# Variance scalings on VectorE, split powers, and new piece orders for four engines in a fused four-layer kernel

## The chip, the cores and the metric

The kernel runs on one core of one Trainium2 chip. The metric is the device time of one execution in microseconds (us), lower is better. Engines are named as the profile names them: PE (TensorE matmuls), PEld (its weight loads), DVE (VectorE), ACT (ScalarE), POOL (GpSimd), SP (SyncE, which issues most of the DMAs).

## The reference

Sixteen sequences of 256 rows and 256 columns go through four layers, each followed by a layer norm of the sum of the layer's input and its output:

```
x = _layernorm(x + _L0_attn_ref(x, ...))   # state-space layer: projections, chunked decay scan, gate, W_out
x = _layernorm(x + _L0_ffn_ref(x, ...))    # int weights minus 128, times a scale; silu(gate) * up, down
x = _layernorm(x + _L1_attn_ref(x, ...))   # below
x = _layernorm(x + _L1_ffn_ref(x, ...))    # top 4 of 16 experts, softmax weights
...
qkv = _rms(x) @ w_qkv.T
q, k, v = jnp.split(qkv, 3, axis=-1)
q = _rms(q)
k = _rms(k)
w = jnp.exp(k)
kv_cum = jnp.cumsum(w * v, axis=1)
w_cum = jnp.cumsum(w, axis=1)
y = jax.nn.sigmoid(q) * (kv_cum / (w_cum + 1e-06))
uv = y @ w_swiglu.T
u, g = jnp.split(uv, 2, axis=-1)
return x + u * jax.nn.silu(g) @ w_out.T
```

## The kernel before

Three blocks run one after the other: the **layers** (three layers and the routing of the fourth, one sequence after another), the **experts** (144 tiles of 128 gathered rows through the 16 experts), and the **combination** (the last layer norm). The change touches the layers only.

In the layers each engine has its own instruction stream, cut into named pieces. `run_skewed` issues the pieces in the order that the table `ORDER` gives for the engine, once per round; round i works on sequence i in the pieces A and F, on i+1 in the pieces with a "+", on i-1 in the pieces B, on i-2 in C and on i-3 in D ("D8+" is i-2, "A6-" is i-1). Rounds 3 to 14 are a hardware loop, the others are written out. The engines meet only through semaphores, so a piece that waits holds up everything behind it in its own stream. What the pieces hold, as far as they are spoken of:

- **G1, G2, G3, G4** (sequence i+1): the first projections (PE), their copies and activations (ACT; G4 is the Silu into `xs`, G3 a logarithm), and the step sizes (DVE; G4.0, G4.1, G4.2 end in `d_a`, `ld`, `q`).
- **A2, A2R, A2L, A3, A3L, AV**: angles `ang`, the sum `g` (which POOL needs for `xg`), rotation, decay factors, masks. On POOL, A2 makes `xg` (128x1024), SP stores it, **AX.0** and **AX.1** gather four and three row selections back into `xgs`, and A2L starts `y`.
- **AU.n, A4.n, AY.n** (n = 0 to 7): one level of the scan each; DVE makes `u` (AU), PE multiplies by the mask (A4), DVE scales the product into `v` (A4) and adds it to `y` (AY, two instructions).
- **A5, A6, A6L**: squares of `y` (ACT), the power on POOL, gating on DVE, transposes and output projection on PE, statistics and normalised rows `x1` (A6L, line 1379).
- **F3, B1, B2**: gate projection `z`; the quantised layer: B1.j multiplies x1T by slices of `w_gate` and `w_up` into `pb`, ACT takes Silu into `sg`, DVE multiplies into `hT` (line 1385); B2 is the down projection. B1T, B3T and B5T are transposes of rows.
- **B2 and B2L** on DVE and POOL: sum `r2`, mean and variance `mv2`; POOL makes two scalings of the variance and one power over both (lines 1078 to 1081); DVE writes `x2n` and `x2` (line 1401). POOL's B3 makes the roots for q and k and negates the one for q (line 1088), which ACT uses as the scale of an exponential.
- **B3, B3V, B4, B5, B6, B6L**: the third layer; B5.j and B6 are its wide projections, B6L writes `x3`.
- **C7, C7L, C8**: `x3` split into two bf16 halves (POOL), logits, the best four experts (DVE, ending in `chosen`), counts (PE's C8), weights and slots (DVE's C8); D8 scatters them to memory (POOL, eight DMAs).
- **WH.k, WL.k**: pieces of the experts' weights, split into high and low halves (ACT, DVE) and stored by SP, one expert per round.

## Time and profile before

| | us |
|---|---|
| median of 3 runs | 2051.54 (2042.37 to 2051.62) |
| the profiled execution, its own time | 2046.18 |
| its span, first to last instruction | 2044.3 |

What the layers, experts and combination take of the span: to about 1427 us the layers, to about 1970 the experts, then the combination. The profile comes in several views: busy time of each engine in a stretch, with the granted TensorE clock (1.00 is 2.4 GHz, 0.50 is 1.2 GHz), and timelines, in which the number in square brackets is how long the engine stood idle before an instruction and who ended that. A timeline merges neighbouring instructions of a kind; "x2" is how many. A matmul in float32 shows as two records.

### The profile page before, as it was taken

What the parts mean: (1) busy time and instruction counts of PE and PEld (TensorE: products, weight loads), DVE (VectorE), ACT (ScalarE), POOL (GpSimd) and SP (SyncE); (2) the same over time, 40 slices, a digit from 0 to 9 for tenths busy, and PEclk for the clock granted to TensorE, in tenths of its full rate; (3) what the DMA queues carried; (4) which work ended last, traced back from release to release, by engine and by line L of the source; (5) the groups of instructions that cost most, each with busy time, mean ns of one, the idle gap of its engine ahead of it and who ended that gap; (6) DMA issues with size and microseconds to landing.
All of it is one profiled execution on the core that took longest, in us unless ns stands there. A gap on an engine that the chain in (4) does not pass through costs nothing. (4 is left out here: it accounts for less than half of the span.)

```text
span 2044.3 us, 34756 instructions
## 1 busy us (share of the span) xinstructions
PE 1763.1 (86%) x8580; PEld 1215.4 (59%) x8581; DVE 1328.9 (65%) x3020; ACT 730.0 (36%) x1384; POOL 854.8 (42%) x855
## 2 busy tenths in 40 slices
PE   3589999999999899998999998873889999999980
PEld 2257667666576676665766766653455566666650
DVE  4678878788788787787888887522344444444445
ACT  3234344344343443444434434221222233232323
POOL 2023243332432433334324333222466676776754
PEclk7799999999999999999999999977899999999995
DMA  5423132231331322313313223162999999999997
GB/s 201 148 94 106 35 110 72 77 109 39 99 109 29 109 70 78 109 39 99 108 30 114 72 71 105 31 273 96 230 158 153 168 172 168 168 171 167 172 142 249
DMA packets 369672, 242.79 MB, mean 119 GB/s; under 512 B 250640, under 2 KB 348240, under 8 KB 369232
## 3 DMA queue, kind: packets, MB, share of 16 engines
q1 hardware_dynamic: 303824, 170.22, 31.5%
q0 software_dynamic: 40704, 67.40, 17.2%
q10 hardware_dynamic: 25088, 4.50, 1.2%
q8 instruction: 26, 0.43, 0.1%
q14 instruction: 30, 0.25, 0.0%
HBM read 121.33 MB, written 68.78 MB: 93 GB/s over the span
## 5 line engine op out<-in xcount | busy, mean ns | idle before, releaser
L1675 PE MATMUL pu<-w_all,xh 128*128 x1728 | 364.3, 358 | 56.4 <-DMA xh<-xin 40.2
L1675 PEld LDWEIGHTS pu<-w_all,xh 128*128 128x128 bf16 x1728 | 169.2, 99 | 209.2 <-issue 92.2
L1806 POOL DMA_INDIRECT sums_dram<-yo,meta_in x144 | 227.8, 1582 | 140.2 <-issue 71.6
L1758 DVE TENSOR_TENSOR hid<-pu,gate 128x448 f32<-128x448 f32 x144 | 89.9, 625 | 255.8 <-PE pu L1675 133.9
L838 PE MATMUL pb<-x1T,w_sw 128*128 128x256 f32 x1024 | 231.2, 384 | 0.7 <-ACT x1T L956 0.7
L838 PEld LDWEIGHTS pb<-x1T,w_sw 128*128 128x128 f32 x1024 | 194.2, 192 | 46.2 <-issue 15.5
L1690 PE MATMUL py<-w_all,hh 128*128 x1584 | 198.4, 275 | 3.0 <-DMA hh<-hs 3.0
L1690 PEld LDWEIGHTS py<-w_all,hh 128*128 128x128 bf16 x1584 | 156.1, 99 | 45.3 <-issue 4.2
L1793 POOL DMA_INDIRECT xin<-x_dram,meta_in x144 | 142.2, 988 | 65.4 <-issue 47.0
L652 PE MATMUL pa<-w_in,xT 128*128 128x512 f32 (+1 forms) x384 | 154.5, 547 | 9.2 <-DMA bc_bias<-in_bc_bias 8.5
L1327 DVE SCALAR_TENSOR_TENSOR y<-v,small,y 128x512 f32<-128x512 f32 x224 | 157.7, 745 | 1.2
L1736 ACT ACTIVATE hs<-hid 128x448 bf16<-128x448 f32 x144 | 83.0, 576 | 197.2 <-DVE hid L1758 160.1
L1143 POOL DMA_INDIRECT meta_dram<-meta,slot x128 | 131.7, 1029 | 49.2 <-issue 43.1
L1727 ACT ACTIVATE gate<-pu 128x448 f32<-128x448 f32 x144 | 78.2, 543 | 194.2 <-PE pu L1675 143.6
L1108 POOL DMA_INDIRECT xgs<-xg_dram,chosen_rows x112 | 115.1, 1028 | 55.3 <-issue 34.4
L1044 POOL TENSOR_SCALAR yss<-yss 128x2 f32<-128x2 f32 x16 | 3.6, 225 | 310.2 <-ACT sq_a L943 310.2
L734 PE MATMUL pa<-u,masked 128*128 128x512 f32 x224 | 113.5, 613 | 19.6 <-DVE masked L1277 14.6
L996 ACT ACTIVATE sg<-pb 128x256 f32<-128x256 f32 x128 | 49.0, 383 | 203.7 <-PE pb L838 201.6
L1773 DVE TENSOR_SCALAR yo<-py,meta_in 128x256 f32<-128x256 f32 x144 | 69.6, 483 | 74.9 <-PE py L1690 44.7
L1314 DVE TENSOR_TENSOR v<-pa,decay 128x512 f32<-128x512 f32 x128 | 84.9, 684 | 51.1 <-PE pa L734 48.6
L652 PEld LDWEIGHTS pa<-w_in,xT 128*128 128x128 f32 x384 | 74.1, 197 | 71.2 <-issue 55.6
L847 PE MATMUL pb<-w_so,hT 128*128 128x256 f32 x512 | 113.1, 379 | 0.0
(244 smaller groups left out, 3196.3 us busy)
## 6 DMA issues: line engine op xcount, KB each, us to landing
w_stage<-in_w_ug SPq DMA_DIRECT2D x64, 224.0 KB
split_ug<-w_parts SPq DMA_DIRECT2D x64, 224.0 KB
w_all<-split_ug SPq DMA_DIRECT2D x16, 896.0 KB, 9.8
xg_dram<-xg SPq DMA_DIRECT2D x16, 512.0 KB, 3.5
w_stage<-in_w_dn SPq DMA_DIRECT2D x32, 256.0 KB
split_dn<-w_parts SPq DMA_DIRECT2D x32, 256.0 KB
w_all<-split_dn SPq DMA_DIRECT2D x16, 512.0 KB, 10.8
rows<-sums_dram SPq DMA_DIRECT2D x32, 256.0 KB, 5.4
```

Of the source, the lines that this page charges most:

```text
L652: last = mm(pa[:, bank + t, 0:width], xT[:, c, t * P:(t + 1) * P], w_in[:, c, first:first + width], start=c == 0, stop=c == DC - 1)
L734: mm(pa[:, n % 2, :], weights, u[:, n % US, :], start=True, stop=True).then_inc(level_done.sem, 1)
L838: last = mm(pb[:, 1 + j % 2, w * T:(w + 1) * T], w_sw[:, c, o:o + P], x1T[:, c, :], start=c == 0, stop=c == DC - 1)
L847: last = mm(pb[:, 3, t * D:(t + 1) * D], hT[:, j, t * P:(t + 1) * P], w_so[:, j, :], start=j == 0, stop=j == SJ - 1)
L1108: nc.gpsimd.indirect_dma_start(out=xgs[:, k, :], out_offset=None, in_=xg_dram, in_offset=bass.IndirectOffsetOnAxis(ap=chosen_rows[:, k:k + ...
L1143: nc.gpsimd.indirect_dma_start(out=meta_dram, out_offset=bass.IndirectOffsetOnAxis(ap=slot[:, t, j:j + 1], axis=0), in_=meta[:, t, j, :], ...
L1327: vec.scalar_tensor_tensor(y[:, t, :], v[:, n % 2, :], small[:, o:o + 1], y[:, t, :], ALU.mult, ALU.add).then_inc(y_added.sem, 1)
L1675: last = mm(pu[:, 2 * b + w, 0:EH], xh[:, m % XS, DC * xp + c, :], w_ug[:, bass.ds(e, 1), wp, c, w * EH:(w + 1) * EH], start=n == 0, stop= ...
L1690: last = mm(py[:, m % 2, 0:D], hh[:, m % XS, b, :], w_dn[:, bass.ds(e, 1), wp, b % EJ, :], start=n == 0, stop=n == EB + EJ - 1)
L1758: vec.tensor_tensor(hid[:, :], pu[:, 2 * (m % 2), 0:EH], gate[:, :], ALU.mult).then_inc(hid_ready.sem, 1)
L1793: nc.gpsimd.indirect_dma_start(out=xin[:, b, :], out_offset=None, in_=x3_dram, in_offset=bass.IndirectOffsetOnAxis(ap=meta[:, m, 1:2], axis=0)
L1806: nc.gpsimd.indirect_dma_start(out=sums_dram[m % 2], out_offset=bass.IndirectOffsetOnAxis(ap=meta[:, m, 0:1], axis=0), in_=yo[:, m % XS, : ...
```

## The change

- The scalings of the three variances leave POOL: DVE adds the small constant (`statistics`) or makes both scalings (DVE's B2) right behind its own statistics, and POOL only raises to the power. For x2n and x2 POOL does two powers of two elements each, x2n's first, and signals each.
- DVE's B2L writes x2n only; x2 is a piece of its own, B2M.
- The columns of `w_qkv` that make q are negated once at the start (DVE, behind sequence 0), and POOL's negation in B3 is gone.
- DVE's `g` is a piece of its own (A2G); routing's slots stay in C8, its weights become C9; POOL's D8 still waits for both.
- Semaphores are merged (`weights_made`, `padding_stored`), so that a chain of its own (`dve_c`) for routing has one.
- ORDER is new for PE, ACT, POOL and DVE; SP's is the same. On ACT, G4+ stands behind B5.1 instead of ahead of B5T, G3+ between B5.4 and B5.5 instead of behind B5.7, and C7L ahead of A2S. On POOL, C7 comes first, A2L's `y` stands between AX.0 and AX.1, and G1+ behind D8+.

```diff
-DVE_G, DVE_A, DVE_B = 10, 10, 16
+DVE_G, DVE_A, DVE_B, DVE_C = 10, 11, 9, 9
...
-    "POOL": ("A6- A2 A2L AX.0 AX.1 C7 B2 G1+ B3 D8+ A5 B6"),
+    "POOL": ("C7 A6- A2 AX.0 A2L AX.1 B2 B3 D8+ G1+ A5 B6"),
...
-            def deviation(chain, norm, mv, s):
+            def deviation(norm, mv, s):
                 pool.wait_ge(norm[0].sem, norm[0].at(s))
                 carrier.take()
-                chain.step(nc.gpsimd.tensor_scalar(mv[:, :, 1:2], mv[:, :, 1:2], 1e-5, None, ALU.add))
                 nc.gpsimd.tensor_tensor(mv[:, :, 1:2], mv[:, :, 1:2], power[:, 0:NT].unsqueeze(2), ALU.pow
...
-                nc.gpsimd.tensor_scalar(scales[:, 0:NT], mv2[:, :, 1], 1.0, LN_EPS, ALU.mult, ALU.add)
-                pb_.step(nc.gpsimd.tensor_scalar(scales[:, NT:2 * NT], mv2[:, :, 1], 1.0 + RMS_EPS, RMS_EPS * LN_EPS,
-                                                 ALU.mult, ALU.add))
-                nc.gpsimd.tensor_tensor(scales[:, :], scales[:, :], power[:, :], ALU.pow).then_inc(norm2[1].sem, 1)
+                for o in (NT, 0):
+                    nc.gpsimd.tensor_tensor(scales[:, o:o + NT], scales[:, o:o + NT], power[:, 0:NT], ALU.pow
+                                            ).then_inc(norm2[1].sem, 1)
...
-                pb_.step(root_mean(pb_, qk_ss[:, :, :].rearrange("p t m -> p (t m)"), D, RMS_EPS))
-                carrier.take()
-                nc.gpsimd.tensor_scalar(qk_ss[:, :, 0:1], qk_ss[:, :, 0:1], -1.0, None, ALU.mult
-                                        ).then_inc(qk_rms_ready.sem, 1)
+                root_mean(pb_, qk_ss[:, :, :].rearrange("p t m -> p (t m)"), D, RMS_EPS).then_inc(qk_rms_ready.sem, 1)
...
+            def a2_g(s):
                 vec.tensor_tensor(g[:, :, :], ld[:, :, :], pa[:, 2, 0:2 * H].rearrange("p (t h) -> p t h", t=NT),
                                   ALU.add).then_inc(g_ready.sem, 1)
...
+                    vec.tensor_scalar(w_qkv[:, :, 0:D], w_qkv[:, :, 0:D], -1.0, None, ALU.mult).then_inc(weights_made.sem, 1)
...
+            def statistics(chain, src, stats, mv, norm):
+                chain.step(moments(chain, src, stats, mv))
+                vec.tensor_scalar(mv[:, :, 1:2], mv[:, :, 1:2], LN_EPS, None, ALU.add).then_inc(norm[0].sem, 1)
...
-                statistics(cb_, r2, st2, mv2, norm2)
+                cb_.step(moments(cb_, r2, st2, mv2))
+                vec.tensor_scalar(scales[:, 0:NT], mv2[:, :, 1], 1.0, LN_EPS, ALU.mult, ALU.add)
+                vec.tensor_scalar(scales[:, NT:2 * NT], mv2[:, :, 1], 1.0 + RMS_EPS, RMS_EPS * LN_EPS,
+                                  ALU.mult, ALU.add).then_inc(norm2[0].sem, 1)
+
+            def normalised_twice(s, o, to, done):
+                dve.wait_ge(norm2[1].sem, norm2[1].at(s, 2 if o == 0 else 1))
+                for t in range(NT):
+                    vec.tensor_scalar(to[:, t, :], r2[:, t, :], mv2[:, t, 0:1], scales[:, o + t:o + t + 1],
+                                      ALU.subtract, ALU.mult).then_inc(done.sem, 1)
```

What the new orders move is shown at three places of the loop's body. The first is DVE's stream at the start of a round: the angles, `g`, the rows x1 of sequence i-1 (`x<-r,mv`), and the search for the best experts from `top` to `chosen`. Before:

```order
L1238 TENSOR_SCALAR ang<-ang 128x128
L1239 TENSOR_TENSOR g<-ld,pa 128x128
...
L1379 TENSOR_SCALAR x<-r,mv 128x256 x2
L1250 TENSOR_TENSOR bct<-bcn,cs 128x256
...
L1260 TENSOR_TENSOR coef<-ld,cb 128x128
L1451 MAX top<-logits 128x8 x2
...
L1466 TENSOR_REDUCE chosen<-hot 128x32
```

The same stretch of the changed kernel:

```order
L1231 TENSOR_SCALAR ang<-ang 128x128
...
L1379 TENSOR_SCALAR x<-r,mv 128x256 x2
L1460 MAX top<-logits 128x8 x2
...
L1475 TENSOR_REDUCE chosen<-hot 128x32
L1234 TENSOR_TENSOR g<-ld,pa 128x128
L1245 TENSOR_TENSOR bct<-bcn,cs 128x256
...
L1255 TENSOR_TENSOR coef<-ld,cb 128x128
```

`g` and the whole rotation moved behind x1 and the search. On PE the counts that need `chosen` moved with it, from behind B1.0 to directly behind B1T.

The second place is PE around the transposes of x2n, B3T (line 757): line 790 is B2, line 734 the scan levels A4, line 652 G1+, line 803 the q and k projection. Before:

```order
L790 MATMUL pb<-w_down,hT 128x256 x7
L734 MATMUL pa<-u,masked 128x512
L734 MATMUL pa<-u,masked 128x512
L652 MATMUL pa<-w_in,xT 128x288 x4
L757 MATMUL pb<-ident,x2n 128x128 x4
L803 MATMUL pb<-w_qkv,x1T 128x512 x4
```

The same stretch of the changed kernel:

```order
L790 MATMUL pb<-w_down,hT 128x256 x7
L652 MATMUL pa<-w_in,xT 128x288 x4
L734 MATMUL pa<-u,masked 128x512
L757 MATMUL pb<-ident,x2n 128x128 x4
L734 MATMUL pa<-u,masked 128x512
L803 MATMUL pb<-w_qkv,x1T 128x512 x4
```

One of the two scan levels moved between the transposes and the projection that needs their copy.

The third place is PE at the end of a round: B5's last slices (line 838), B6 (line 847), the transposes of y, A5 (line 740), and the output projection A6 (line 746). Before:

```order
L838 MATMUL pb<-x1T,w_sw 128x256 x4
L847 MATMUL pb<-w_so,hT 128x256 x7
L847 MATMUL pb<-w_so,hT 128x256 x9
L740 MATMUL pa<-ident,y 128x128 x8
L746 MATMUL pa<-w_out,ynT 128x256 x8
```

The same stretch of the changed kernel:

```order
L838 MATMUL pb<-x1T,w_sw 128x256 x4
L847 MATMUL pb<-w_so,hT 128x256 x7
L847 MATMUL pb<-w_so,hT 128x256
L740 MATMUL pa<-ident,y 128x128 x4
L847 MATMUL pb<-w_so,hT 128x256 x8
L740 MATMUL pa<-ident,y 128x128 x4
L746 MATMUL pa<-w_out,ynT 128x256 x8
```

The first half of A5 moved between the halves of B6.

## Rows read from the trace of the kernel before

**Rows 1.** Windows: us, busy PE PEld DVE ACT POOL, then clock, DMA share, GB/s.
```profile
662.95:745.05 82.10, 76.33 (x331) 54.88 (x330) 65.21 (x146) 33.84 (x66) 29.05 (x33) 0.98 0.26 80
```
**Rows 2.** Timeline of DVE: the sum r1, once per round (start us, us, ...).
```profile
258.68 0.69 DVE L1341 TENSOR_TENSOR r<-x_row,pa 128x512 f32<-128x512 f32 x1 [0.74 <-PE pa L746]
...
1321.83 0.69 DVE L1341 TENSOR_TENSOR r<-x_row,pa 128x512 f32<-128x512 f32 x1 [0.74 <-PE pa L746]
```
**Rows 3.** Timeline of PE, one round: the places where it stood idle.
```profile
664.09 3.72 PE L746 MATMUL pa<-w_out,ynT 128*128 128x256 f32 x16 [0.31 <-ACT ynT L949]
...
674.41 0.66 PE L757 MATMUL pb<-ident,x 128*128 128x128 f32 x4 [0.49 <-DVE x L1379]
...
679.64 0.18 PE L867 MATMUL pb<-chosen,count_mats 128*128 128x16 bf16 x1 [0.84 <-DVE chosen L1466]
...
682.53 1.13 PE L776 MATMUL pb<-x1T,w_gate 128*128 128x256 f32 x4 [0.41 <-DVE hT L1385]
...
691.74 6.03 PE L790 MATMUL pb<-w_down,hT 128*128 128x256 f32 x24 [1.03 <-DVE hT L1385]
...
703.06 0.66 PE L757 MATMUL pb<-ident,x2n 128*128 128x128 f32 x4 [1.43 <-DVE x2n L1401]
704.40 5.40 PE L803 MATMUL pb<-w_qkv,x1T 128*128 128x512 f32 x8 [0.69 <-ACT x1T L956]
...
714.43 0.70 PE L820 MATMUL pb<-wv,const 128*128 128x256 f32 x2 [0.34 <-ACT eq L987]
```
**Rows 4.** Windows within that round, and timeline of PE in a later round.
```profile
705.02:706.04 1.02, 1.02 (x2) 0.34 (x1) 1.02 (x3) 1.01 (x3) 0.73 (x2) 0.50 0.00 0
...
1032.64 3.70 PE L803 MATMUL pb<-w_qkv,x1T 128*128 128x512 f32 x8 [0.69 <-ACT x1T L956]
```
**Rows 5.** Timelines of DVE and of POOL, the same round's start.
```profile
671.97 2.38 DVE L1379 TENSOR_SCALAR x<-r,mv 128x256 f32<-128x256 f32 x2
...
676.44 0.25 DVE L1451 MAX8 top<-logits 128x8 f32<-128x16 f32 x2
...
677.14 1.44 DVE L1457 TENSOR_TENSOR ez<-top 128x8 f32<-128x8 f32 x1
...
672.22 1.98 POOL L1095 TENSOR_TENSOR xg<-xs,g 128x1024 f32<-128x1024 f32 x1 [1.20 <-DVE g L1239]
676.60 1.96 POOL L1115 TENSOR_TENSOR y<-xs,coef 128x1024 f32<-128x1024 f32 x1 [2.40 <-DVE coef L1260]
```
**Rows 6.** Timelines of POOL and of DVE between the variance and x2n.
```profile
665.57 0.71 POOL L1051 TENSOR_TENSOR mv<-mv,power 128x2 f32<-128x2 f32 x1
...
699.52 0.25 DVE L1373 BATCH_NORM_AGGREGATE mv<-st 128x2 f32<-128x6 f32 x2
...
702.26 0.73 DVE L1401 TENSOR_SCALAR x2n<-r,mv,scales 128x256 f32<-128x256 f32 x2 [1.21 <-POOL scales L1081]
...
680.38 0.17 DVE L1479 TENSOR_SCALAR tok<-tok 128x2 f32<-128x2 f32 x1
```
**Rows 7.** Timeline of ACT in B1: the late sg.
```profile
690.69 0.83 ACT L966 ACTIVATE sg<-pb,s_gu 128x256 f32<-128x256 f32 x2 [3.93 <-PE pb L776]
```
**Rows 8.** Gathers: timelines of SP, of POOL, and of both POOL and DVE in round 0.
```profile
676.01 0.37 SPq L615 DMA_DIRECT2D xg_dram<-xg  x1
...
680.14 1.09 POOL L1108 DMA_INDIRECT xgs<-xg_dram,chosen_rows  x1 [1.58 <-DMA xg_dram<-xg]
...
39.74 0.95 POOL L1108 DMA_INDIRECT xgs<-xg_dram,chosen_rows  x1 [0.30 <-issue]
...
47.09 1.90 DVE L1305 TENSOR_TENSOR u<-xgs,from_first 128x512 f32<-128x512 f32 x3 [8.96 <-DMA xgs<-xg_dram,chosen_rows]
```
**Rows 9.** Timelines of ACT, DVE and PE at the round's end.
```profile
738.54 1.28 ACT L902 ACT_TABLE_LOAD   x1
...
742.83 1.41 DVE L1334 SCALAR_TENSOR_TENSOR y<-y,yss,zs 128x512 f32<-128x512 f32 x2
...
737.94 7.07 PE L847 MATMUL pb<-w_so,hT 128*128 128x256 f32 x32
```

More of the change, by code:

```diff
@@ L1394, in b2, with b2_second @@
                                            ALU.add))
[L1395 to L1402 removed]
+                cb_.step(moments(cb_, r2, st2, mv2))
[7 more added lines that the diff above has]
+                                      ALU.subtract, ALU.mult).then_inc(done.sem, 1)
+            def b2_late(s):
+                normalised_twice(s, NT, x2n, x2n_ready)
+            def b2_second(s):
+                normalised_twice(s, 0, x2, x2_ready)
             def b3(s):
@@ L1439, in b6 @@
                 statistics(cb_, r2, st2, mv2, norm3)
+                cb_.end()
             def b6_late(s):
@@ L1446, in c7_late @@
             def c7_late(s):
-                cb_.go_on(s)
+                cc_.start(s)
                 dve.wait_ge(logits_copied.sem, logits_copied.at(s))
@@ L1451, in c7_late @@
                     last = vec.max(top[:, t, :], logits[:, t, :])
-                cb_.step(last)
+                cc_.step(last)
                 carrier.take()
@@ L1463, in c7_late @@
                                              spread(topf[:, t, :], 2, NE), ALU.is_equal)
-                cb_.step(last)
+                cc_.step(last)
                 with nc.allow_low_precision(reason="sums of at most one one are exact"):
@@ L1469, in c8, with c9 @@
             def c8(s):
-                cb_.go_on(s)
+                cc_.go_on(s)
+                dve.wait_ge(counted.sem, counted.at(s))
+                cc_.step(vec.tensor_tensor(pos[:, :, :], pb[:, 3, 0:NT * NE].rearrange("p (t e) -> p t e", t=NT),
+                                           spread(base[:, :], 1, NT), ALU.add))
+                vec.tensor_tensor(base[:, :], base[:, :], pb[:, 3, NT * NE:(NT + 1) * NE], ALU.add)
+                for t in range(NT):
+                    last = vec.tensor_tensor(hot_pos[:, t, :, :], hot[:, t, :, :], spread(pos[:, t, :], 1, TOPK), ALU.mult)
+                cc_.step(last)
+                cc_.step(vec.tensor_reduce(slot_f[:, :, :], hot_pos[:, :, :, :], AX_X, ALU.add))
+                if later(s):
+                    dve.wait_ge(meta_stored.sem, meta_stored.before(s))
+                flat = "p t j -> p (t j)"
+                vec.scalar_tensor_tensor(slot[:, :, :].rearrange(flat), topf[:, :, :].rearrange(flat), float(cap),
+                                         slot_f[:, :, :].rearrange(flat), ALU.mult, ALU.add
+                                         ).then_inc(meta_ready.sem, 1)
+            def c9(s):
+                cc_.go_on(s)
                 dve.wait_ge(top_exp.sem, top_exp.at(s))
-                cb_.step(vec.tensor_reduce(esum[:, :], ez[:, :, :], AX_X, ALU.add))
-                cb_.step(vec.reciprocal(esum[:, :], esum[:, :]))
+                cc_.step(vec.tensor_reduce(esum[:, :], ez[:, :, :], AX_X, ALU.add))
+                cc_.step(vec.reciprocal(esum[:, :], esum[:, :]))
                 if later(s):
```

84 lines of the change are left out of this document (32 added, 52 removed), and 17 rows, old and new, of the table ORDER.

## The prediction

> **What bounds the kernel now.** I read first the windows. In one round of the layers, 82.10 us long, PE is busy 76.33 us and DVE 65.21, at a granted clock of 0.98 [rows 1]. So PE sets the round, and what can be won is what PE waits and what it loses at the lower clock. The sum r1 marks the rounds: from 258.68 to 1321.83 us there are 13, 81.8 us each [rows 2], and two more lie before them. The experts and the combination are not touched and have no piece of the layers beside them, so they move as a whole.
>
> Next the timeline of PE through one round, where the reader is to see every idle time and its releaser [rows 3]: 0.31 (ACT's copy of y's transposes), 0.49 (x1), 0.84 (`chosen`), 0.41 (the first `hT`), 1.03 (a late `hT`), 1.43 (x2n), 0.69 (the copy of x2n's transposes), 0.34 (the exponential of q): 5.5 us. Then the clock: right behind the 2.1 us of idleness around x2n the q and k projection takes 5.40 us, and the window inside it shows 0.50, that is 1.2 GHz; in a later round the same eight records take 3.70 at full clock [rows 3, 4]. That is 1.7 us more. It happens in 10 of the 13 rounds.
>
> **The change, part by part**, as us per round.
>
> *x1 and g.* Today `g` comes first, POOL's xg starts at 672.22 and lasts 1.98, and DVE's two x1 instructions take 2.38 instead of the 0.73 of the equal x2n pair [rows 5, 6]. With `g` behind the search, xg can't start there: x1 is ready 1.65 us earlier, PE's 0.49 goes. What is late next is PE's own gate projection. The price moves to the rotation, which then stands beside xg for up to 1.98 us. PE needs the rotated B and C only behind B1.1, two slices of eight 256-column records later; 0.43 us is a 512-column record at full clock (3.70/8 less its tail), so a slice is 1.73. That covers it: nothing.
> The row shows that a tensor_scalar of DVE stood still while POOL read SBUF. The Trainium skill (SBUF — State Buffer, Who interferes with whom) says the same of instructions of DVE with two SBUF inputs, and that who starts first keeps the port for the whole instruction; by it xg's and y's 2 us fall upon the rotation and on `u`, never away, and the gain would be nil if PE waited for those. The rows of this kernel say that it doesn't for the rotation; for `u` it is part of the second and third rivals.
>
> *`chosen`.* The search starts at 676.44, its `ez` takes 1.44 beside POOL's y, and PE waits until 679.64 [rows 3, 5]. Without that blocking (at least 1.2 us) it takes 3.2 - 1.2 = 2.0. Behind x1, from about 672.6, it ends near 674.6, when PE has done B1T (674.41 less 0.49 and 0.5 of work, 674.4). The 0.84 shrinks to 0.2 at most; ACT gets to the first `sg` earlier too (its table loads follow one another without the wait for `ez`), which takes the 0.41. Gain 0.84 + 0.41 - 0.2 = 1.05.
>
> *The late hT.* PE's 1.03 comes from an `sg` that ACT starts only at 690.69, 3.93 us after its last work, though its matmuls ended near 687.9 [rows 3, 7]. No piece ahead of it explains that; it coincides with the gathers. I keep the 1.03: bounds 0 (stays) and 1.03 (goes).
>
> *x2n.* From the variance (699.52 + 0.25) to x2n (702.26) it is 2.49 us: two scalings and one power over four elements [rows 6]. Now DVE adds two tensor_scalars on tiny operands, 0.17 each of which about 0.1 counts, with one step wait: 0.3. POOL wakes 0.2 later and needs 0.71 for a power over two elements [rows 6]: 1.25 in all. Gain 1.2 on the path to B3T. One scan level (0.86) leaves the cover ahead of B3T, so the 1.43 stays at about 1.1, but it comes to stand in the 0.69: from B3T to the projection the copy takes 704.40 - 703.06 = 1.34, of which 0.5 is transposes and 0.86 the level. So the projection starts 1.2 us earlier. x2 in its own piece costs nothing: only the next round's x1 and B6 read it.
>
> *The clock.* Idleness there falls from 2.1 to 1.1 us in one piece, with dense records on both sides. All other waits of the round, up to 1.03 us, left the clock at 1.00. I take the full 1.7 in the 10 rounds that have it; bounds 0 and 1.7.
> The Trainium skill (TensorE: Matmul & The Clock Gate, Part 1) describes a gate that rests at half rate and is released by activity. The trace agrees with two levels; by the rule alone a remaining 1.1 us wait may keep the fall; the sum would then be 3.4 a round, which is the first rival.
>
> *q's sign.* One POOL instruction and its step wait go from a chain that PE waits 0.34 for; two scan levels and B3V still cover it. Gain 0.34 [rows 3]. The negation at the start costs DVE about 0.4 us once.
>
> *The end of the round.* B6.0, A5.0, B6.1, A5.1, A6: ACT's copy of the first half now lies beside B6.1 (3.5 us), so the 0.31 goes. But the first half of y must be normalised by the end of B6.0. Today B6 starts at 737.94, half of its 7.07 ends at 741.5, and the gating starts at 742.83, done 0.7 later [rows 9]: 2 us too late. The new orders pull A4.7 and AY.7 ahead of B5.6 and of G4.1's reciprocal, put ACT's squares ahead of B5.7, and move G4.2 behind the gating. On DVE AU.7, AY.2 and AY.3 stand ahead of B5.0 and WL.4 behind A5, so that it has room. Counting DVE's and ACT's pieces from the exponential on, I get the gating about 0.5 us ahead of need. G3's logarithm now sits between two Silus, and costs ACT two table loads of 1.28 [rows 9] where one was; ACT is idle half of the time there.
>
> *The rest.* POOL's C7 first costs the x1 power nothing, since x3 is ready before x1's variance. POOL's eight scatters ahead of G1+ end some 2 us before DVE's G4.0 wants the root. SP's order is the same.
>
> Sum per round: 0.49 + 1.05 + 1.2 + 0.34 + 0.31 = 3.4, and 1.7 where the clock falls: 5.1. Over 15 rounds: 15 x 3.4 + 10 x 1.7 = 68. In the drain after 1321.83, where nothing covers the chains, x2n (1.2), the negation (0.3) and x3's scaling (0.3) give 2 us more. Each wait that goes takes the pipeline's tail with it (about 0.1, three us in all). From 2046.2 of the profiled execution (span 2044.3 and 1.9 around it): **1973 us**. The runs' median, 2051.5, is 5 above that execution; three rounds that kept the full clock in the one and lost it in the others are 3 x 1.7 = 5, and with the fall gone both start from the same place.
>
> **The rivals.**
> 1. *The clock still falls.* For: a wait of 1.1 remains at the same place. Against: it is half as long. 12 to 15 rounds x 1.7: 1973 + 20 to 25 = 1995.
> 2. *The end of the round becomes the bound:* y isn't gated by B6.0's end, or DVE, busy 65 of what would be 77 us, is late with `hT`. For: the margin of 0.5. Each us is 15: with 1.5, 1995; with the first rival, 2016.
> 3. *The gathers, slower than before.* xg ends 2.5 us later (near 676.8); from SP's issue to the first gather it was 4.1 us [rows 8], so AX.0 starts near 681.1 and its fourth issue (0.95 + 0.30 each) ends near 686. DVE's AU.0 comes at 687.5, ahead of B1.5, and PE's B2 wants that hT at 690.7, two `u` later. So data may land 3 us behind the last issue; with the port taken by y (1.96) that is about what is there. In round 0, beside the weights' loads, it was 47.09 - 40.69 = 6.4 [rows 8]: then PE waits 3.4 us per round, 51 us in all, 2024. It turns slower than before beyond 3 + 5 = 8 us; at 9 it gives some 2062. Against: in the loop the DMAs are at a quarter load.
> 4. *More is won:* the late `sg` goes as well, 15 x 1.03, and the tails count double: 1973 - 15 - 3 = 1955. That the change doesn't do what it says is excluded for the scalings (POOL's instructions are gone) and small for the rest.
>
> **How the numbers follow.** Forecast (1960 to 1988) 0.50; clock 0.18; end of round, alone or with the clock, 0.16; gathers late but still faster 0.04, slower 0.03; more won 0.09. The range goes from below the fourth rival to the second with the first, 1946 to 2016, and leaves out the late gathers and what no row told me of. A measurement here tells 0.5%, about 10 us, from no change. Faster by more: all but the gathers' slow part and a little unforeseen: 0.93; same 0.03, slower 0.04.
>
> **What would show it.** Right: r1's distance near 76.7 us; no 0.50 in the window of the q and k projection; x1 in 0.73 us; PE waits for `chosen` and ynT gone; x2n's wait near 1.1; B6's halves without a wait between. Wrong: DVE waiting for `xgs` ahead of B1.5, PE waiting for y at A5.0, or a new idle time of PE behind ACT's Silu at B5.5. A round of 79 or more would say that DVE or ACT took over.

## The result and the profile after

The changed kernel takes **1956.6 us** (median of 4, 1956.2 to 1958.5), the kernel before 2047.2 beside it (median of 4, 2042.4 to 2051.6): ratio 0.956, 95% interval 0.953 to 0.959. Forecast were 1973.0, with a range of 1946 to 2016.

The views of the changed kernel answer to the rows of before as follows. First its windows over one round (columns as in [rows 1]):

```profile
625.87:701.97 76.10, 74.48 (x330) 54.20 (x331) 64.51 (x150) 35.38 (x67) 28.59 (x29) 1.00 0.28 86
```

The round went from 82.1 to 76.1 us and PE's busy time from 76.33 to 74.48 at an unbroken clock. So of the 6.0 about 1.9 is busy time, 1.7 of it the clock's, and 4.1 is idle time. Next, PE's timeline from the end of B2 to the first scans, against the 1.43, 0.69 and 5.40 of [rows 3]:

```profile
653.36 2.21 PE L652 MATMUL pa<-w_in,xT 128*128 128x288 f32 x8
655.40 1.02 PE L734 MATMUL pa<-u,masked 128*128 128x512 f32 x2
657.45 0.66 PE L757 MATMUL pb<-ident,x2n 128*128 128x128 f32 x4 [1.02 <-DVE x2n L1403]
657.94 1.02 PE L734 MATMUL pa<-u,masked 128*128 128x512 f32 x2
658.80 3.69 PE L803 MATMUL pb<-w_qkv,x1T 128*128 128x512 f32 x8
```

The one wait that is left here is 1.02; the projection runs at full clock. The chain that ends it, on DVE and POOL, against [rows 6]:

```profile
655.18 0.25 DVE L1369 BATCH_NORM_AGGREGATE mv<-st 128x2 f32<-128x6 f32 x2
655.46 0.17 DVE L1396 TENSOR_SCALAR scales<-mv 128x2 f32<-128x2 f32 x1
655.54 0.16 DVE L1397 TENSOR_SCALAR scales<-mv 128x2 f32<-128x2 f32 x1
656.65 0.73 DVE L1403 TENSOR_SCALAR x2n<-r,mv,scales 128x256 f32<-128x256 f32 x2 [0.95 <-POOL scales L1076]
...
655.88 1.54 POOL L1076 TENSOR_TENSOR scales<-scales,power 128x2 f32<-128x2 f32 x2 [5.75 <-DVE scales L1397]
```

From the variance's end (655.43) to x2n it is 1.22 us; it was 2.49. The start of the round on DVE and PE, against [rows 3, 5]:

```profile
629.98 0.73 DVE L1379 TENSOR_SCALAR x<-r,mv 128x256 f32<-128x256 f32 x2
...
632.11 0.37 DVE L1475 TENSOR_REDUCE chosen<-hot 128x32 bf16<-128x128 f32 x1
...
632.92 2.20 DVE L1246 TENSOR_TENSOR bcu<-bcn,cs 128x256 f32<-128x256 f32 x1
...
632.54 0.18 PE L867 MATMUL pb<-chosen,count_mats 128*128 128x16 bf16 x1
```

x1 takes 0.73, `chosen` is there when PE gets to it, and the slow instruction beside xg is now one of the rotation, `bcu`, which nobody waits for.

To compare whole executions I cut them into rounds at the end of PE's last up projection of B1, and summed within each round the pauses between PE's records above 0.1 us (**waits**). What remains (**rest**) is work, at the clock it had. The first of these cuts is the **first mark**, the sixteenth is the last; 15 rounds lie between them, the first and the last of which are the outer ones. A **fall** is a stretch in which the granted clock is 0.50. The means of the 13 inner rounds, in us:

| kernel | round | waits | rest | first mark |
|---|---|---|---|---|
| before, first traces | 81.35 | 5.43 | 75.92 | 120.9 |
| after, first traces | 75.93 | 1.49 | 74.44 | 113.1 |
| before, with the experiments | 80.29 | 4.79 | 75.50 | 121.3 |
| after, with the experiments | 75.75 | 1.33 | 74.42 | 109.5 |

The rest is two-valued: in the trace of before with the experiments 76.3 in seven inner rounds and 74.6 in six, the 1.7 of [rows 3, 4]; after has 74.4 in all. In the first pair the 87.6 us of the spans are 13 x 3.94 = 51 of waits, 13 x 1.48 = 19 of rest, 7.8 up to the first mark, 7.7 in the two outer rounds, and 1.6 behind the last mark. Of these 1.6, 1.3 lie in the experts (559.0 to 557.7 us), whose code is the same; the layers' own part behind the last mark is as long as before (70.4 and 70.6).

### The profile page after: what moved, and what is told of

Read it like the earlier page. It is cut to its first block and busy times, and to the rows that moved or that the text cites. A ratio compares the mean times of both kernels' runs of the same rounds, so it can differ in the third digit from the quotient of the medians.

```text
span 1956.7 us, 34760 instructions
## 1 busy us (share of the span) xinstructions
PE 1740.7 (89%) x8580; PEld 1208.8 (62%) x8581; DVE 1320.4 (67%) x3085; ACT 751.6 (38%) x1398; POOL 844.3 (43%) x791
## 5 line engine op out<-in xcount | busy, mean ns | idle before, releaser
L652 PE MATMUL pa<-w_in,xT 128*128 128x512 f32 (+1 forms) x384 | 159.8, 562 | 23.5 <-DVE masked L1272 14.2
L1102 POOL DMA_INDIRECT xgs<-xg_dram,chosen_rows x112 | 122.1, 1091 | 93.0 <-DMA xg_dram<-xg 47.7
L652 PEld LDWEIGHTS pa<-w_in,xT 128*128 128x128 f32 x384 | 74.6, 201 | 84.7 <-issue 68.4
L776 PE MATMUL pb<-x1T,w_gate 128*128 128x256 f32 (+1 forms) x384 | 103.5, 392 | 0.8 <-DVE w_down L1360 0.4
L847 PEld LDWEIGHTS pb<-w_so,hT 128*128 128x128 f32 x512 | 95.0, 190 | 13.6
```

Source lines behind the costliest of these rows:

```text
L652: last = mm(pa[:, bank + t, 0:width], xT[:, c, t * P:(t + 1) * P], w_in[:, c, first:first + width], start=c == 0, stop=c == DC - 1)
L776: last = mm(pb[0:rows, 1 + j % 2, w * T:(w + 1) * T], weight[:, c, j * P:j * P + rows], x1T[:, c, :], start=c == 0, stop=c == DC - 1)
L847: last = mm(pb[:, 3, t * D:(t + 1) * D], hT[:, j, t * P:(t + 1) * P], w_so[:, j, :], start=j == 0, stop=j == SJ - 1)
L1102: nc.gpsimd.indirect_dma_start(out=xgs[:, k, :], out_offset=None, in_=xg_dram, in_offset=bass.IndirectOffsetOnAxis(ap=chosen_rows[:, k:k + ...
```

## The experiments

All runs beside the kernel before, which takes 2031 us there (2047 in the first comparison). "Control" is the changed kernel. e5, e6, e8 and e10 ran on another chip than the control and the other experiments; the kernel before takes 2032 there, 1.3 more, and the control was not run on it.

The experts' part, from its first matmul to its last, has the same code in all kernels and takes 548.9 to 559.3 us in the 14 traces. That puts a scatter of 10 us into the totals; its cause is open. So each total is read beside the time of the last mark, which only the layers set (one trace each, difference to the control in brackets): control 1251.3; e1 1269.8 (+18.5); e2 1299.6 (+48.3); e3 1291.4 (+40.1); e4 1264.3 (+13.0); e5 1254.1 (+2.8); e6 1301.0 (+49.7); e8 1254.7 (+3.4); e9 1261.7 (+10.4); e10 1341.4 (+90.1); before 1325.8; e7 1318.2.

### Controls

No edit.

> The changed kernel, unedited, beside the experiments on their chip, so that they are compared with it there. The kernel before takes 2031 us on the chip of the first four experiments against 2047 in the first comparison. Theory A (the difference between chips lies in how often the clock falls and how often the fifth sg comes late before): the changed kernel has neither and takes its 1957 us here too, within 4. Theory B (everything scales): 1957 x 2031 / 2047 = 1942 us.

> The kernel before, unedited, for a trace of it from the chip of the experiments. In the first trace the ten rounds with the clock's fall took 76.4 us without TensorE's waits and the others 74.8, and the fifth sg was over 2 us late in nine rounds. If this chip's 2031 us are the same rounds with fewer falls, about (2047 - 2031) / 1.6 = 10 rounds fewer fall, that is nearly none; if the late sg is what differs, TensorE's waits in the down product (0.9 us in those nine rounds) are gone and the falls stay.

Measured: after **1952.9** (ratio 0.963, 0.959 to 0.967), before 2029.5. The control's theory A holds: after moved by 4 us only, while before moved by 16. The trace of before shows both causes that its expectation names. It has the fall in 7 inner rounds where it had 9 of 13 in the first trace, and the late `sg` in none:

```profile
677.59 0.47 ACT L966 ACTIVATE sg<-pb,s_gu 128x256 f32<-128x256 f32 x1 [1.25 <-PE pb L776]
679.32 0.47 ACT L966 ACTIVATE sg<-pb,s_gu 128x256 f32<-128x256 f32 x1 [1.25 <-PE pb L776]
682.05 0.47 ACT L966 ACTIVATE sg<-pb,s_gu 64x256 f32<-64x256 f32 x1 [2.26 <-PE pb L776]
```

These are three Silus of ACT in one round, each right behind its matmuls; in [rows 7] the fifth one had waited 3.93. PE's wait for `hT` at B2, 0.73 in the mean of the inner rounds then, stands in two of them here (0.48 and 0.60). So with the same code the late `sg` comes in the first comparison and not here, and the same holds of after: 0.5 us late in eleven rounds of the first trace, never here. The record does not name the chip of the first comparison, so that a difference between chips is likely but not shown. Of the 16 us by which the two `before` differ, 13 x 0.64 = 8 are waits and 13 x 0.42 = 5 rest.

### e1: the arithmetic back on POOL

```
-                vec.tensor_scalar(scales[:, 0:NT], mv2[:, :, 1], 1.0, LN_EPS, ALU.mult, ALU.add)
-                vec.tensor_scalar(scales[:, NT:2 * NT], mv2[:, :, 1], 1.0 + RMS_EPS, RMS_EPS * LN_EPS,
...
+                nc.gpsimd.tensor_scalar(scales[:, 0:NT], mv2[:, :, 1], 1.0, LN_EPS, ALU.mult, ALU.add)
+                pb_.step(nc.gpsimd.tensor_scalar(scales[:, NT:2 * NT], mv2[:, :, 1], 1.0 + RMS_EPS, RMS_EPS * LN_EPS,
...
+                nc.gpsimd.tensor_scalar(qk_ss[:, :, 0:1], qk_ss[:, :, 0:1], -1.0, None, ALU.mult)
```

The other two variances' additions go back to POOL as well. What stays from the change is the split power, x2n's first, and x2 as a piece of its own.

> The changed kernel with its new orders, but the variance scalings, the additions of epsilon and the negation of q's factors done on GpSimd again, as before. Theory A (the arithmetic carries a part of the gain, the orders the rest): TensorE's wait for x2n is 1.02 us with the change; two or three GpSimd operations of 0.54 to 0.60 us and a power of 1.04 in place of 0.71 stand in the chain again, so it grows to about 2.2, that is 1.2 x 15 rounds = 18 us; q's sign gives back 0.34 x 15 = 5 us at the wait for eq; and if the longer wait takes TensorE's clock down again (query and key products 5.4 in place of 3.69 us) another 1.7 x up to 14 = 24. Sum +23 to +47 us over the changed kernel's 1956.6, that is 1980 to 2004. Theory B (the orders do it all, the chain of x2n has slack now): under +5 us, at most 1962, the wait for x2n as before this edit, and the products at 3.69 us throughout.

Measured: **1965.1**, 12.2 above the control; rounds of 76.68, waits 2.38, rest 74.31, no fall. Up to the last mark it is 18.5 more, and the experts take 6.2 less. So theory A without its clock part (23) is near in the sum. It is not in the terms: x2n's wait grew by 0.27 a round, not 1.2; two short waits at the start of the round (0.14, and 0.23 for ACT's `zs`) and 4.0 us ahead of the first mark were not in it. POOL and PE in one round:

```profile
661.24 0.19 POOL L1078 TENSOR_SCALAR scales<-mv 128x2 f32<-128x2 f32 x1 [5.66 <-DVE mv L1378]
661.49 0.19 POOL L1079 TENSOR_SCALAR scales<-mv 128x2 f32<-128x2 f32 x1
...
663.33 0.66 PE L757 MATMUL pb<-ident,x2n 128*128 128x128 f32 x4 [1.30 <-DVE x2n L1408]
...
673.11 0.70 PE L820 MATMUL pb<-wv,const 128*128 128x256 f32 x2 [0.44 <-ACT eq L987]
```

POOL's scalings take 0.19 each here, not 0.53 and 0.54. What stands beside them in the kernel before (its trace with the experiments, POOL and DVE):

```profile
690.17 0.53 POOL L1078 TENSOR_SCALAR scales<-mv 128x2 f32<-128x2 f32 x1 [7.80 <-DVE mv L1373]
690.77 0.54 POOL L1079 TENSOR_SCALAR scales<-mv 128x2 f32<-128x2 f32 x1
...
689.97 1.29 DVE L1305 TENSOR_TENSOR u<-xgs,from_first 128x512 f32<-128x512 f32 x2
```

Two wide `u` of DVE lay over POOL's small instructions. The new order took AU.4 and AU.5 out from between B2 and B2L. So the path to x2n was shortened three times: by the order, by the split power and by moving the scalings. The waits go from 1.43 + 0.69 = 2.12 to 1.29 in e1 (order and split power), to 0.49 + 0.69 = 1.18 in e2 below (split power and moved scalings), to 1.02 with all three. POOL's part up to x2n's power falls from 2.26 us to 1.26 in e1; 0.69 of that is the two scalings without `u` over them, 0.31 the power (1.04 over four elements, 0.73 over two). The order was not run alone against this wait: e1 still has the split power. The Trainium skill (SBUF — State Buffer, Who interferes with whom) has the shared port of DVE and POOL; these rows agree for a two-input instruction of DVE, 0.54 against 0.19. In these rows `u` had started 0.2 us ahead of POOL's instruction; where POOL's root starts 0.1 ahead of a `u`, in the control, it keeps its 1.01.
q's sign costs 0.44 at `eq` where I had 0.34.

### e2: the arithmetic alone, in the old order

The table `ORDER` of before, with DVE's `A2 A2G`, `C8 C9` and `B2L B2M` next to each other, so that each pair does what one piece did.

> The changed kernel's arithmetic (scalings on VectorE, x2n's power apart, queries negated once) in the order of pieces of the kernel before. Theory A (orders and arithmetic each carry their own part and add): the start of the state space part (x1 and the chosen rows, 1.3 us a round) and the late sg (about 0.9 us in 10 rounds) come back, 15 x 1.3 + 10 x 0.9 = 29, the first round's wait for the weight pieces 5.5, sum +34 us, 1991; where the clock falls again in the query and key products another 1.7 x 10 = 17, 2008. Theory B (the arithmetic carries nearly all, since the clock's fall followed from the chain of x2n): under +12 us, below 1969, all products at 3.7 us.

Measured: **2006.1**, 53 above the control. These are theory A's mechanisms in part: it had 1991 without the clock, and its 2008 needed falls and a late `sg`, neither of which came. That the result is near 2008 is chance. PE, one round:

```profile
760.18 0.65 PE L756 MATMUL pb<-ident,x2n 128*128 128x128 f32 x4 [0.49 <-DVE x2n L1402]
761.52 3.70 PE L802 MATMUL pb<-w_qkv,x1T 128*128 128x512 f32 x8 [0.69 <-ACT x1T L955]
...
801.20 3.72 PE L745 MATMUL pa<-w_out,ynT 128*128 128x256 f32 x16 [0.31 <-ACT ynT L948]
...
811.75 0.66 PE L756 MATMUL pb<-ident,x 128*128 128x128 f32 x4 [0.72 <-DVE x L1378]
...
816.99 0.18 PE L866 MATMUL pb<-chosen,count_mats 128*128 128x16 bf16 x1 [0.85 <-DVE chosen L1474]
...
819.92 1.13 PE L775 MATMUL pb<-x1T,w_gate 128*128 128x256 f32 x4 [0.45 <-DVE hT L1384]
```

0.31 + 0.72 + 0.85 + 0.45 = 2.3 us per round are the orders' share, 35 us over 15 rounds (theory A had 1.3 a round), and 12.4 us more come before the first mark, for which I had 5.5. The projection never leaves 3.70 in the 13 rounds (rest 74.51): **the arithmetic with the split power ends the clock's fall by itself**, though the same two waits stand there, shorter. e1, with the order and the split power, ends it too.

### e3: g first again

```
-    "DVE": ("A2 A6L- C7L A2G A2R C8 ...
+    "DVE": ("A2 A2G A6L- C7L A2R C8 ...
```

> The changed kernel with one VectorE piece moved: g (which lets GpSimd begin the product xg) ahead of x1's normalisation, as before. Theory A (x1's tensor_scalar is slow while GpSimd's product runs, 2.38 us beside it and 0.73 without): x1 takes some 2.4 us again and TensorE's waits for x1 and the chosen rows return, 0.5 to 1.3 us a round, +7 to +20 us, 1964 to 1977, while the gathers start some 0.7 us sooner. Theory B (the slowness of x1 came from elsewhere, or the earlier gathers pay for it): x1 stays at 0.73 us or the time within 3 us of the changed kernel, 1954 to 1960.

Measured: **2003.6** (1988.9 to 2005.5; the profiled execution is the fastest): 36 to 51 us above the control, more than theory A. The trace can account for the 36 only. DVE, POOL and PE in one round:

```profile
803.60 2.38 DVE L1379 TENSOR_SCALAR x<-r,mv 128x256 f32<-128x256 f32 x2
...
817.17 3.47 DVE L1280 TENSOR_TENSOR decay<-decay,alpha 128x896 f32<-128x896 f32 x1
...
803.85 1.98 POOL L1089 TENSOR_TENSOR xg<-xs,g 128x1024 f32<-128x1024 f32 x1 [1.50 <-DVE g L1234]
...
817.70 1.98 POOL L1109 TENSOR_TENSOR y<-xs,coef 128x1024 f32<-128x1024 f32 x1
...
806.04 0.66 PE L757 MATMUL pb<-ident,x 128*128 128x128 f32 x4 [0.51 <-DVE x L1379]
...
807.80 0.18 PE L867 MATMUL pb<-chosen,count_mats 128*128 128x16 bf16 x1 [1.11 <-DVE chosen L1475]
...
822.12 1.08 PE L776 MATMUL pb<-x1T,w_gate 128*64 128x256 f32 x4 [1.81 <-DVE hT L1385]
```

One piece moved, and x1 takes exactly its old 2.38 beside xg. With it PE's 0.51 and 1.11 return. Beyond that POOL's y, which in the new order follows the four gathers, falls on DVE's `decay`: 2.67 to 3.47 us, where the changed kernel has 1.08 at 641.88, and PE waits up to 1.81 for `hT`. In the rows above `decay` had started 0.53 ahead of y and was held all the same, so who starts first does not decide here. Nor do the gathers start sooner against xg: they come 6.0 to 6.6 us behind its end, in the changed kernel 4.0 in nearly every round, since SP's queue has two loads ahead of xg's store, and the first of them starts 0.2 us behind x1 (806.16 here, 630.89 in the changed kernel).

The clock falls once in this trace, behind a single wait for `hT`:

```profile
427.98 1.23 PE L776 MATMUL pb<-x1T,w_gate 128*64 128x256 f32 x4 [1.63 <-DVE hT L1385]
```

```profile
428.80:432.20 3.40, 3.40 (x9) 1.87 (x8) 2.00 (x5) 0.47 (x1) 1.35 (x1) 0.50 0.84 200
```

The rounds with 1.60 and 1.81 at this place kept the clock. The other four executions, 14 to 17 us longer, have mean clocks of 0.949 to 0.953 against 0.955, so more of these falls are a likely part of them; they have no trace.

### e7: before with the new order on POOL alone

```
-    "POOL": ("A6- A2 A2L AX.0 AX.1 C7 B2 G1+ B3 D8+ A5 B6"),
+    "POOL": ("C7 A6- A2 AX.0 A2L AX.1 B2 G1+ B3 D8+ A5 B6"),
```

> The kernel before with only GpSimd's order of pieces changed to the new one in its first part (copies of x3 in two parts first, then xg, the gathers parted by y's product). Theory A (the late sg of the feed forward's fifth block, 2.1 to 2.7 us in 9 rounds before, hangs on what GpSimd does beside it, since with GpSimd's new order it is 0.5): it falls to 0.6 us or less, TensorE's waits in the down product go from 0.9 to 0.3 or less in those rounds, -6 us, and up to -17 more where TensorE's clock then holds: 2025 to 2041. Theory B (the late sg follows from the orders of the other engines): it stays at 2.1 to 2.7 us, and the time is within 4 us of before's 2047, or above it, since the product xg starts 1.8 us later behind the copies.

Measured: **2025.3**, ratio 0.997 (0.995 to 0.9996). For its question it is void: c_before shows that before has no late `sg` in this company, so that its absence here says nothing. What it does show is the price of parted gathers where they are not in step with the rest. PE in one such round, and the windows behind its wait (clock, third number from the end) and behind the same wait of another round, 1.66 there:

```profile
762.20 3.68 PE L790 MATMUL pb<-w_down,hT 64*128 64x256 f32 x14 [1.62 <-DVE hT L1385]
```

```profile
762.20:766.00 3.80, 3.80 (x15) 2.60 (x16) 3.40 (x4) 0.00 (x0) 0.00 (x0) 1.00 0.08 31
445.10:448.50 3.40, 3.40 (x9) 2.68 (x10) 2.58 (x4) 0.00 (x0) 0.00 (x0) 0.50 0.00 0
```

DVE had waited 3.34 us for `xgs`. Three such rounds take 82.2 to 82.9. In two the fall stands behind this wait (2.28 and 1.66), in the third only behind x2n's. The others take 78.0 to 80.1, one of them with a fall behind x2n's waits. What makes the `sg` late in the first comparison stays open.

### e4, e5, e6: what takes the clock down

Only PE's order is touched, at the wait for x2n.

```
 after: G1+ A4.0 B3T A4.1 B3.0 B3.1
 e4:    G1+ B3T A4.0 A4.1 B3.0 B3.1
 e5:    G1+ A4.0 A4.1 B3T B3.0 B3.1
 e6:    G1+ B3T B3.0 A4.0 A4.1 B3.1
```

> The changed kernel with one TensorE piece moved: x2n's transposition ahead of the first state product instead of behind it, so that TensorE waits for x2n in one stretch of 1.02 + 0.86 = 1.9 us. Both theories have the wait itself: +0.86 x 15 = 13 us, 1970. Theory A (the clock falls when TensorE's idle time in this stretch passes what it is with the change; before, 1.43 + 0.69 us with the fall in 10 of 15 rounds): the query and key products go to 5.4 us in most rounds, 1.7 x 10 to 15 more, 1987 to 1996. Theory B (one wait of 1.9 us is no cause; the fall came with the waits ahead of it in the down product): the products stay at 3.7 us, 1966 to 1972.

> The changed kernel with the second state product moved ahead of x2n's transposition, so that the two waits of the kernel before stand there again, shorter: 0.16 us for x2n and 0.69 us for its transposed copy, 0.85 in place of 1.02. Theory A (time in this stretch is TensorE's idle time and nothing else): 0.17 x 15 = 2.6 us less than the changed kernel's 1952.9 on this chip, 1950. Theory B (two waits close together are what takes the clock down, as the 1.43 + 0.69 us before): the query and key products go to 5.4 us in some rounds, +1.7 us for each, 1957 to 1975.

> The changed kernel with x2n's transposition and the first projection of queries and keys ahead of both state products, so that nothing covers the two waits: 1.88 us for x2n and 0.69 us for its copy, 2.6 us of idle time within 3.3 us, more than the 2.1 us of the kernel before at the same place. Both theories have the idle time: +1.55 x 15 = 23 us, 1976. Theory A (the clock falls by the sum of idle time in this stretch; 2.12 us before with a fall in half of the rounds, 1.9 us in one piece with a fall in one round of fifteen): it falls in nearly every round, the products 5.4 us, 1.7 x 15 = 25 more, 2001. Theory B (it takes the other waits of a round as well, which the kernel before has and this one has not): no falls, 1974 to 1979.

PE in one round of e4, then of e6:

```profile
660.09 0.66 PE L757 MATMUL pb<-ident,x2n 128*128 128x128 f32 x4 [1.88 <-DVE x2n L1403]
660.58 1.88 PE L734 MATMUL pa<-u,masked 128*128 128x512 f32 x4
```

```profile
676.76 0.66 PE L757 MATMUL pb<-ident,x2n 128*128 128x128 f32 x4 [1.88 <-DVE x2n L1403]
678.10 3.78 PE L803 MATMUL pb<-w_qkv,x1T 128*128 128x512 f32 x4 [0.69 <-ACT x1T L956]
```

In e6 four records of the projection take 3.78, as long as eight take at full clock, and the window around them has a granted clock of 0.78:

```profile
674.00:680.00 6.00, 3.44 (x11) 1.66 (x10) 2.88 (x13) 3.29 (x6) 1.54 (x2) 0.78 0.00 0
```

| | waits around x2n | measured | inner rounds with a fall there | mean rest |
|---|---|---|---|---|
| e5 | 0.16 + 0.69 | 1952.5 | 0 | 74.60 |
| control | 1.02 | 1952.9 | 0 | 74.42 |
| e2 | 0.49 + 0.69 | 2006.1 | 0 | 74.51 |
| e1 | 1.29 | 1965.1 | 0 | 74.31 |
| e4 | 1.88 | 1970.8 | 0 | 74.35 |
| before | 1.43 + 0.69 | 2029.5 | 7 of 13 | 75.50 |
| before, first comparison | 1.43 + 0.69 | 2047.2 | 9 of 13 | 75.92 |
| e7 | 1.43 + 0.69 | 2025.3 | 2 of 13, 2 more elsewhere | 75.00 |
| e6 | 1.88 + 0.69 | 2002.8 | 11 of 13 | 76.30 |

e4 is its theory B: up to the last mark +13.0, the 13 of the wait alone, and 4.1 in the experts. Its one fall is in the first outer round, where the wait was 2.08. Theory B's reason, that the fall comes with the waits ahead in the down product, does not hold: five of the seven inner rounds of before that fell had no such wait. e5: no fall, theory A, but its 2.6 us are within the scatter, and its inner rounds are as long as the control's (75.76 and 75.75): the waits went down by 0.17 and the rest up by as much. e6 is theory A, and 1.8 from the number. So at this place the falls grow with the idle time: none in the inner rounds up to 1.88 us in one piece, 2 to 9 of 13 at 2.1 in two, most at 2.6, three of them (rest 77.6) with more than one share of 1.7. The first inner round of before and e7 has 1.24 + 0.69 = 1.93 there, and fell in one of three traces. One wait of 1.88 was tried, not two that sum to it, so length and division are not told apart.

The length of the idle time is not the whole cause. At other places the clock fell behind single waits of 1.66 (e7) and 1.63 (e3), shorter than e4's 1.88, and before has rounds with equal waits of which one falls and the next does not. What decides between them no run here shows.

### e8: the fourth weight piece put back

```
-   ACT:  ... G2+ WH.2 B3 B3L B5T ... B5.2 WH.3 WH.4
+   ACT:  ... G2+ WH.2 WH.3 B3 B3L B5T ... B5.2 WH.4
-   DVE:  ... A4.3 B4E ... B5.2 WL.3 A4.5
+   DVE:  ... A4.3 WL.3 B4E ... B5.2 A4.5
```

> The changed kernel with the fourth weight piece put back to where it stood: on ScalarE right behind the third, ahead of the gate and silu work, on VectorE ahead of the attention part. Theory A (before, the first round stood for it: ScalarE waited 17 to 18 us for the down projection's piece to land, VectorE 6.4 to 7.3 for ScalarE; the changed kernel reaches the first down product 11.8 us sooner on this chip): 5 to 8 us of these return in the first round, 1958 to 1961, the later rounds as in the changed kernel, 75.7 us. Theory B (the gain of the first rounds comes from the other pieces that moved): within 1.5 us of 1952.9.

Measured: **1958.1** (1954.5 to 1963.7), first mark at 111.3. That is within theory A's range, but not by its mechanism: the first mark did not come back to 121. The trace has PE waits of 0.2 to 0.5 us for `hT` in five inner rounds and 1.6 at the end of the thirteenth. The edit was at fault: I had counted the pieces wrongly. ACT in the first round, kernel before and then the changed one, both with the experiments:

```profile
75.57 0.63 ACT L1017 ACTIVATE w_parts<-w_stage 128x512 bf16<-128x512 f32 x1 [18.01 <-DMA w_stage<-in_w_dn]
76.21 1.28 ACT L909 ACT_TABLE_LOAD   x1
77.51 1.08 ACT L909 ACTIVATE xs<-pa 128x512 f32<-128x512 f32 x2
```

```profile
66.95 1.09 ACT L909 ACTIVATE xs<-pa 128x512 f32<-128x512 f32 x2
...
75.29 0.63 ACT L1017 ACTIVATE w_parts<-w_stage 128x512 bf16<-128x512 f32 x1 [6.79 <-DMA w_stage<-in_w_dn]
```

The piece that waits for `in_w_dn` is WH.4, the fifth. Before, it stood ahead of G4+ on ACT and held `xs` for 10.6 us; now it stands behind it. On DVE WL.4 stood ahead of a part of AY, and DVE waited for it 7.30 us. That this is the gain of the first rounds is read from the traces and fits all runs: the first mark is at 121 to 122 in the four traces with ACT's old order (before twice, e2, e7), and at 109.5 to 115 in the ten with the new. WH.4 alone was not tried, and ACT's old order never ran without the old orders of PE and DVE.

### e9, e10: fill the last wait

e9 puts A4.0, A4.1 ahead of B3T and A4.2 behind it, and DVE's A4.0 ahead of G1+. e10 also takes A4.5 ahead of B4.0 and A4.6 behind B5T, and moves DVE's A4.3 and A4.4 forward to match.

```
 PE after: G1+ A4.0 B3T A4.1 B3.0 B3.1 A4.2 B3V A4.3 A4.4 B4.0
 PE e9:    G1+ A4.0 A4.1 B3T A4.2 B3.0 B3.1 B3V A4.3 A4.4 B4.0
 PE e10:   G1+ A4.0 A4.1 B3T A4.2 B3.0 B3.1 B3V A4.3 A4.4 A4.5 B4.0
```

> The changed kernel with two more state products of TensorE between the end of the down product and x2n's use (first and second ahead of x2n's transposition, the third behind it), and VectorE's use of the first ahead of the gate work, so that the third finds its memory free. Theory A (the wait of 1.02 us for x2n is plain idle time): 0.16 us of it is left, and the 0.69 us behind the transposition stays hidden by the third product if VectorE frees its memory 0.7 us after x2n; 15 x 0.86 = 13 us less, 1944. Theory B (the time is only moved: TensorE waits for the third product's memory or VectorE's later pieces come later and stop it in the values' part): within 4 us of the changed kernel, or up to 15 us more if VectorE's delayed gate work of 1.4 us a round is waited for.

> The experiment with the third state product behind x2n's transposition, and the sixth moved too, ahead of the cumulative products of keys and values, where TensorE then waited 1.41 us for eq; the seventh takes its place behind yc's transposition. Theory A (the time for the chain from the feed forward's end to eq is fixed, about 14 us, and every product of 0.86 us put into it takes 0.86 us from its waits): the wait for eq goes to 0.55, x2n's stays 0.16; 0.86 x 15 = 13 us less than that experiment's 1964.1, 1951, and 2 us below the changed kernel. Theory B (VectorE, which has to free one more accumulator in that stretch, becomes the one waited for, or the attention part's products wait for want of the moved ones): 1955 or more.

Measured: e9 **1964.1**, e10 **2039.7**. PE of e9 at x2n and `eq`, and then of e10 behind the move:

```profile
658.15 0.66 PE L757 MATMUL pb<-ident,x2n 128*128 128x128 f32 x4 [0.16 <-DVE x2n L1403]
...
668.21 0.70 PE L820 MATMUL pb<-wv,const 128*128 128x256 f32 x2 [1.41 <-ACT eq L987]
```

```profile
717.00 2.04 PE L734 MATMUL pa<-u,masked 128*128 128x512 f32 x2 [3.89 <-DVE v L1309]
```

In e9 the 0.86 that goes at x2n comes back at `eq`, since A4.2 had covered that chain, and 0.55 on top. The chain itself has grown, as POOL's timeline shows for e9 and then for the changed kernel:

```profile
664.58 0.44 POOL L1044 TENSOR_SCALAR qk_ss<-qk_ss 128x4 f32<-128x4 f32 x1 [6.45 <-ACT sq_b L976]
665.11 1.39 POOL L1045 TENSOR_TENSOR qk_ss<-qk_ss,power 128x4 f32<-128x4 f32 x1
```

```profile
663.71 0.20 POOL L1044 TENSOR_SCALAR qk_ss<-qk_ss 128x4 f32<-128x4 f32 x1 [6.28 <-ACT sq_b L976]
663.99 1.01 POOL L1045 TENSOR_TENSOR qk_ss<-qk_ss,power 128x4 f32<-128x4 f32 x1
```

The root's two instructions take 1.83 in place of 1.21. In e9 DVE's `u` of AU.5 starts 0.3 ahead of the first, and y's additions lie over both; in the control they start behind POOL's. Waits per round 1.84 against 1.33: theory B. In e10 the wait for `eq` is gone, as its A says, but A4.6 needs the buffer that DVE's A4.4 frees, and that stands behind a reciprocal of 3.35 us. PE waits 3.89 there and in all 4.70, the window from 716 to 722 has a clock of 0.53, and the rest rises to 77.26. The control and e5 are the fastest that I found, and e5's last mark is 2.8 later than the control's: nothing beats the changed kernel by more than the scatter.

## Why the prediction was right, step by step

**The bound.** PE bounds the round before and after; DVE didn't take over (64.51 of 76.1 busy).

**The 3.4 per round of waits.** With the experiments' pair it is 4.79 - 1.33 = 3.46. Term by term: x1's 0.49 went, `chosen` and the first `hT` (1.05 forecast, 0.84 + 0.41 = 1.25 gone, since `chosen` ended 0.06 ahead of PE, not 0.2 behind), x2n's path 1.10 of 1.2 (2.12 to 1.02; I had said 1.1 would stay), q's sign 0.34, ynT 0.31. The path itself came out at 1.22 from variance to x2n; the forecast's 0.3 + 0.2 + 0.71 is 1.21, not the 1.25 that it gives. e1 and e2 agree with the last three, with one addition: the x2n chain owed 0.69 of its length to DVE's `u`, which the prediction did not see. It took the length of POOL's scalings as theirs and thought that they must leave POOL to be short. So the size of this term is right with a reason that is right only in part: in the old order the moved scalings and the split power bring it (e2), and the new order with the split power brings most of it without moving them (e1).

**The late `sg`.** This step was wrong in the first pair: I kept PE's 1.03, the fourth rival let it go. PE's wait for `hT` at B2 fell from a mean of 0.73 to 0.15, 0.58 of the 3.94. Not all of it was the late `sg`: two rounds of before had 0.97 and 0.43 without one.

**The fill.** The prediction had no term for the time to the first mark. It gave 7.8 us (11.7 with the experiments). ACT's wait of 17 us in the first round stood in the trace of before, and I had not read the first 120 us engine by engine. This term was missing altogether.

**The sum.** From profiled execution to profiled execution 73 us were forecast and 87.7 measured. The difference of 14.6 has these terms: the fill +7.8, the inner rounds' waits +7.0 (51.2 for 44.2), the inner rounds' rest +3.9 (19.2 for 9 x 1.7), the outer rounds -0.8, behind the last mark -0.4, and the 3 us of tails, which no row shows as such and which may be part of the rest. The result is 16 below the forecast, since the profiled execution is also 1.9 above the median of its four. It stayed in the range, which went down by 27; the fill stood in no rival, so this was in part luck.

**The clock.** Forecast: 1.7 in 10 rounds, none left. (The prediction says 10 of the 13; it is 9 of the 13 inner ones and the first outer one.) Measured: all gone in the inner rounds and the first outer one, mean rest down by 1.48 in the first pair (1.7 x 9/13 = 1.2, and 0.3 that no view explains), 1.08 in the second. The reason given (idle time halved, in one piece) is borne out by e6, and e4 shows that at this place the margin was larger than thought: 1.88 in one piece kept the clock in all inner rounds. But the prediction's supporting argument, that all other waits up to 1.03 us left the clock alone, says nothing of waits between 1.03 and 2.1, and waits of 1.63 and 1.66 at other places did bring it down. That the changed kernel has no such wait but one (1.45, at B2, without a fall) may be part of why the term came true. The Trainium skill (TensorE: Matmul & The Clock Gate, Part 1) has a gate that rests at half rate; the two levels agree, 0.50 and 1.00 here. That rule gives neither the difference between these waits nor the fall at 1.1 us that the prediction drew from it.

**x1 and g.** Right as said and shown by e3: 2.38 beside xg, 0.73 without, the price moved to the rotation (`bcu` 2.20), where it is covered. The size was too small: with the old place of `g` alone it is 36 us and more, not 15 x 1.5, because the later y meets `decay` as well, and because the clock fell once in the trace, likely more often in the other executions. The prediction's rule that who starts first keeps the port fits POOL's root in the control (started 0.1 ahead of `u`, 1.01 us) but not `decay` in e3 (started 0.53 ahead of y, 3.47 for 1.08).

**The end of the round.** Right. The gating began at 692.65 and its first half was done 0.5 ahead of PE's A5.0, the forecast's 0.5. DVE did wait 1.04 us for the Silu behind G3's table loads; the sign that I had named as wrong was a new idle time of PE there, and there was none.

**The gathers.** First gather 4.0 us behind xg's end. DVE waiting for `xgs` ahead of B1.5, a sign that I had named as wrong, came in every round: 0.9 to 1.5 us in twelve inner rounds (1.54 in this one), 2.6 in one, where before had such a wait in three. It reached PE's B2 in three of them only (0.30 in this round, 0.19, and 1.45 in one). Landing took 4.0 us behind the fourth issue (643.04 + 0.94 to 648.02) where 3 were assumed: the third rival's mechanism was near, its price was not reached.
